# Row maxima added to the attention scores by one-hot products on TensorE instead of by a transfer into the stacked operand

## What is computed

```python
x = x + causal_self_attention(layernorm(x))            # no weights, q = k = v
x = x + cross_attention(layernorm(x), ctx, bias)       # bias is (16, 16 heads, 128, 128), added to the scores
x = x + ffn_block(layernorm(x))                        # a second attention, then a mixture of 8 experts, top 1

scores = einsum("bhtd,bhsd->bhts", q, k) + bias        # cross; the ffn block's attention has no bias
probs  = softmax(scores, axis=-1)
attn   = einsum("bhts,bhsd->bhtd", probs, v)
```

## Time and profile before

| | |
|---|---|
| median of 3 runs | 578.4 us (578.15 to 583.85) |
| profiled execution | 579.9 us, its span 578.2 us |
| PE busy | 373.3 us, 65% of the span |
| PE weight loads | 318.1 us, 55% |
| DVE busy | 291.0 us, 50% |
| ACT busy | 202.9 us, 35% |
| POOL busy | 169.9 us, 29% |
| moved by DMA | 82.35 MB, mean 142 GB/s |

### The profile page before, as it was taken

The page is one execution under the profiler, slowest core; times in us unless marked ns, Lnnn a source line. Parts: engine busy times, 40 slices in busy tenths (PEclk is TensorE's granted clock), DMA queues, the critical chain, the costliest instruction groups (busy, mean ns, idle before and its releaser), DMA issues.

```text
span 578.2 us, 11981 instructions
## 1 busy us (share of the span) xinstructions
PE 373.3 (65%) x4299; PEld 318.1 (55%) x4299; DVE 291.0 (50%) x845; ACT 202.9 (35%) x414; POOL 169.9 (29%) x244
## 2 busy tenths in 40 slices
PE   1285666625849696686958966486367395007995
PEld 0164444514638585675857856376356384007995
DVE  4124121215775575755757655545366274404773
ACT  1255444422324232332324333344245163003552
POOL 4222101210122222333334544123123123371543
PEclk9989777777787897987979977857788588557999
DMA  2777677888384856758544433945856421122331
GB/s 76 187 191 201 173 196 214 217 217 215 99 202 128 214 139 174 199 135 217 130 105 116 116 81 103 227 108 131 203 158 156 103 84 47 36 104 68 100 88 39
DMA packets 75335, 82.35 MB, mean 142 GB/s; under 512 B 6171, under 2 KB 61566, under 8 KB 71822
## 3 DMA queue, kind: packets, MB, share of 16 engines
q1 hardware_dynamic: 73774, 78.43, 52.8%
q0 software_dynamic: 1504, 3.16, 1.6%
HBM read 56.20 MB, written 25.51 MB: 141 GB/s over the span
## 4 chain that ended last, share of the span: by engine, by line
DMA 36%; PE 25%; SPq 18%; DVE 10%; issue 5%; POOL 4%; ACT 0%; POOLq 0%; DVEq 0%; ACTq 0%
DMA stack<-maxT 21%; DMA k_scratch<-parts 12%; PE out_bank L524 7%; PE score_bank L524 5%; SPq L257 5%; PE proj_bank L524 4%; PE score_bank L527 3%; PE max_bank L524 3%; SPq L287 3%; POOL routed_rows L507 3%; SPq L266 2%; DVE biased L920 2%; DVE rowmax L924 2%; SPq L253 2%; SPq L269 2%
## 5 line engine op out<-in xcount | busy, mean ns | idle before, releaser
L773 ACT ACTIVATE probs<-score_bank 128x512 f32<-128x512 f32 x192 | 112.2, 598 | 220.4 <-PE score_bank L524 218.7
L524 PE MATMUL score_bank<-stack 74*128 74x128 bf16 (+1 forms) x768 | 111.2, 247 | 49.8 <-DMA stack<-maxT 49.8
L524 PEld LDWEIGHTS score_bank<-stack 74*128 74x128 bf16 (+1 forms) x768 | 74.3, 113 | 64.9 <-issue 57.4
L527 PE MATMUL score_bank<-ident,bias_in 128*128 128x128 f32 x256 | 57.6, 309 | 35.9 <-DMA stack<-maxT 35.9
L524 PE MATMUL out_bank<-probs,vaug 128*32 128x128 f32 x1536 | 68.9, 336 | 0.0
L527 PEld LDWEIGHTS score_bank<-ident,bias_in 128*128 128x128 f32 x256 | 41.1, 161 | 42.1 <-issue 36.1
L429 POOL TENSOR_TENSOR att_sel<-att,in_block 128x1024 f32<-128x1024 f32 x16 | 34.3, 2144 | 89.7 <-DVE att L956 89.7
L524 PEld LDWEIGHTS out_bank<-probs,vaug 128*32 128x32 f32 x1536 | 50.6, 134 | 10.4 <-issue 5.0
L524 PE MATMUL score_bank<-causal,identb 128*128 128x512 bf16 x64 | 29.8, 465 | 40.9 <-DMA stack<-k_scratch 40.9
L381 POOL TENSOR_SCALAR vareps<-meanvar 128x2 f32<-128x2 f32 x32 | 7.1, 223 | 164.4 <-DVE meanvar L869 164.3
L945 DVE COPY maxT<-finish_bank 128x128 bf16<-128x128 bf16 x32 | 7.1, 222 | 93.4 <-PE finish_bank L589 93.4
(11 more groups left out here) (141 smaller groups left out, 642.5 us busy)
## 6 DMA issues: line engine op xcount, KB each, us to landing
k_scratch<-parts SPq DMA_DIRECT2D x72, 192.0 KB, 3.2
stack<-q_scratch SPq DMA_DIRECT2D x24, 576.0 KB
stack<-k_scratch SPq DMA_DIRECT2D x24, 576.0 KB
q_scratch<-parts SPq DMA_DIRECT2D x24, 192.0 KB, 2.9
bias_in<-in_w SPq DMA_DIRECT2D x16, 256.0 KB, 3.9
routed_rows<-filler SPq DMA_DIRECT2D x2, 1028.0 KB, 8.9
vaug<-routed_rows SPq DMA_DIRECT2D x23, 64.5 KB, 1.8
parts<-routed_rows SPq DMA_DIRECT2D x23, 64.0 KB, 2.1
```

Of the source, the lines that this page charges most:

```text
L524: return nc.tensor.matmul(o, lhsT, rhs, start=start, stop=stop, **kw)
L527: return nc.tensor.matmul(o, src, ident[:], start=True, stop=stop, is_transpose=True)
L773: nc.scalar.activation(probs[:, b % 2, g, :], sbk[g % 2][:], ACT.Exp, scale=1.0 if layer(b) == CROSS else SCALE).then_inc(s_p, 1)
```

## The change

The stack keeps its 72 rows; the two rows for the maxima and for ones go, with `max_rows` on SP, the three transfers of ones, and their semaphores. In place of `ones_row` there is `pick`, 128 x 16 x 128 in bf16: for head h it is one in the rows h and h + 16 and zero elsewhere. POOL makes it with a memset and two selects. In `scores`, for each head of a cross or ffn item, a second product follows that of the stack: `pick[:, head, :]` as weights and `maxT[:, b % 2, :]`, all 128 rows of it, as the moving operand, added into the same bank. PE waits for `s_maxT` in place of the transfer's semaphore, and once for `pick`. DVE, before it writes a buffer of `maxT` again, waits for the scores that read it.

```diff
-MROWS = ROWS + 2
-        stack = sb("stack", [MROWS, NSTACK, 2, NH, PAIR], bf16)
+        stack = sb("stack", [ROWS, NSTACK, 2, NH, PAIR], bf16)
-        ones_row = sb("ones_row", [128, PAIR], bf16)
+        pick = sb("pick", [128, NH, S], bf16)
...
-            def max_rows(b):
-                wait(sp, s_maxT, b - B + 1)
-                sp.dma_start(stack[ROWS:MROWS, b // 2 % NSTACK, 0, :, b % 2 * S:(b % 2 + 1) * S],
-                             maxT[0:2 * NH, b % 2, :]).then_inc(s_maxrow[b % 2], 16)
...
-                if b == 6:
-                    sp.wait_ge(s_pool_const, 1)
-                    for i in range(NSTACK):
-                        sp.dma_start(stack[ROWS:MROWS, i, 1, :, :],
-                                     ones_row[0:2, :].unsqueeze(1).to_broadcast([2, NH, PAIR])).then_inc(s_ones, 16)
...
-                if FIRST_CROSS <= b + 1 < NB:
-                    max_rows(b + 1)
...
-            nc.gpsimd.memset(ones_row[:], 1.0).then_inc(s_pool_const, 1)
+            nc.gpsimd.memset(pick[:], 0.0).then_inc(s_pool_const, 1)
...
+                nc.gpsimd.affine_select(out=pick[:], in_=pick[:], compare_op=ALU.not_equal, fill=1.0, base=0,
+                                        pattern=[[-1, NH], [0, S]], channel_multiplier=1).then_inc(s_pool_const, 1)
+                pool.wait_ge(s_pool_const, 13)
+                nc.gpsimd.affine_select(out=pick[:], in_=pick[:], compare_op=ALU.not_equal, fill=1.0, base=-NH,
+                                        pattern=[[-1, NH], [0, S]], channel_multiplier=1).then_inc(s_pool_const, 1)
...
             def scores(b, g):
                 i, s, bk, kind = b // 2 % NSTACK, b % 2, sbk[g % 2], layer(b)
-                depth = ROWS if kind == SELF else MROWS
...
                     if kind != SELF:
-                        pe.wait_ge(s_maxrow[b % 2], 16 * ((b - B) // 2 + 1))
+                        pe.wait_ge(s_maxT, b - B + 1)
                     if b == FIRST_CROSS:
-                        pe.wait_ge(s_ones, 16 * NSTACK)
+                        pe.wait_ge(s_pool_const, 14)
...
-                    last = mm(o, stack[0:depth, i, 1, head, s * S:(s + 1) * S],
-                              stack[0:depth, i, 0, head, s * S:(s + 1) * S], start=kind == FFN,
-                              stop=kind != SELF or h == G - 1)
+                    last = mm(o, stack[:, i, 1, head, s * S:(s + 1) * S], stack[:, i, 0, head, s * S:(s + 1) * S],
+                              start=kind == FFN, stop=kind == SELF and h == G - 1)
+                    if kind != SELF:
+                        last = mm(o, pick[:, head, :], maxT[:, b % 2, :], start=False)
...
             def take_maxT(b):
                 dve.wait_ge(s_mtr, b - B + 1)
-                wait(dve, s_maxrow[b % 2], 16 * ((b - B) // 2))
+                wait(dve, s_e, NG * (b - 1))
                 nc.vector.tensor_copy(maxT[:, b % 2, :], fb[:].bitcast(bf16)[:, 0:128]).then_inc(s_maxT, 1)
```

More of the change, by code:

```diff
@@ L162, in build @@
         s_stack = [sem(f"stack_loaded{i}") for i in range(NSTACK)]
-        s_ones = sem("ones_in_stack")
-        s_maxrow = [sem(f"max_rows_in_stack{i}") for i in range(2)]
         s_pool_const = sem("pool_constants")
```

## The result

| | before | after |
|---|---|---|
| median | 581.1 us (4 runs beside the new ones) | 530.1 us (528.6 to 536.2) |
| ratio | | 0.916, 95% interval 0.905 to 0.927 |
| span of the profiled execution | 578.2 us | 528.9 us |
| mean granted clock of PE | 0.81 | 0.88 |

The account below looks back on a forecast made before the run. The prediction took PE's waits for the late row-maxima transfer into the stack as the bound. Cross -25, FFN -42, rows of ones -1.3, last slots +1 made -67 to -68 from 578.2: 510 us, range 494 to 535.

Parts of the forecast that it names:

- PE is slower than priced: Rival: clock stays at 0.82 to 0.86, all sixteen products count; cross pair 21.5, FFN 15.7, 535 us; chance 0.14.
- FFN stage: Seven pairs of 20.2 us become 14.2 us, PE waiting for the stack some 2 us per pair: 42 us less.
- removed wait in the cross stage: Long slot part falls from 15.33 to 10.0 us; a pair with products takes 19.7 us; eight pairs 25 us less.
- the stack takes over the wait: Rival: earlier bias loads delay the loop's writes and reads; cross pair about 22 us, FFN 17, 550 us; chance 0.13.
- price of the products: 512 added products at 0.056 us each, 28.7 us in all; eight of a slot's sixteen count, 0.45 us per slot.
- depth costs nothing: New products 128 deep cost as much as those 72 deep, since weight loads take 109 ns against 113 ns.
- the circle: PE score maxima, DVE row maxima, PE transpose; in the FFN stage, with products, 12.4 us per pair.
- L = 18.2: FFN loop from exponential through k's write to DRAM and stack read to score maxima: 20.2 us less 2.0.
- P = 14.2: FFN pair in us: two pairs span L + 12.4 - 2.2 = 28.4; 15.2 if L stays, 12.4 if hidden.
- overlap of 2.2 us: FFN stage: PE work from `scores` to the first score maxima at full clock, taken off the loop's two-pair span.
- rows of ones: Start of the kernel: removing three issues on SP gives 1.3 us less (0 to 2).
- Slower: Rival: added products on a PE at half clock; cross pairs 35 us, FFN 26, +90 + 43, 710 us; chance 0.03.

Follow-up runs that it names:

- experiment 3: The changed kernel with a second product, weights of zeros, beside each new one (512 more): 545.6 us, ratio 0.940 to the kernel before.
- Experiment 11: The kernel before, its row-maxima transfer kept, with 512 zero-weight products and the new waits added: 586.3 us, ratio 1.016.
- experiment 12: The changed kernel with the added products cut to 32 rows deep: 691.4 us, ratio 1.174 to the kernel before.
- experiment 1: The changed kernel with its three 1 MB filler writes issued after SP's slot loop: 518.4 us, ratio 0.895 to the kernel before.
- experiment 5: The changed kernel, fillers after the loop, POOL doing `low_parts` before `inverse_deviation` from slot 16 on: 520.5 us, ratio 0.901 to the kernel before.
- experiment 7: The changed kernel, fillers after the loop, POOL doing `low_parts` before `inverse_deviation` from slot 34 on: 513.1 us, ratio 0.879 to the kernel before.
- experiment 8: The changed kernel, fillers in place, POOL doing `low_parts` before `inverse_deviation` from slot 34 on: 525.6 us, ratio 0.904 to the kernel before.
- experiment 9: The changed kernel with 24 products of 512 columns on PE before its stack wait in slots 36, 40, 44: 525.5 us, ratio 0.914 to the kernel before.

## Why the prediction was right or wrong

**The number: in the range, in part by luck.** The forecast's own bounds were 494 to 526, and 530.1 lies above them. The range reaches to 535 because the rival "PE is slower than priced" was taken in, and what made the time longer is for the most part not what that rival said. By the prediction's own sign, FFN pairs above 16 us, its FFN stage is wrong: five of the seven take 16.4 to 22.8 us.

**The bound and the removed wait in the cross stage: right.** The chain named the transfer, and without it a pair takes 19.0 to 19.5 us where the sum said 19.7. The long slot is 10.5 us (sum 10.45), the short one 9.0 (sum 9.3). The clock came back to 1.00. The first two pairs are shorter still (17.2 and 17.7); that is 4.5 us of the 6.5 that were gained beyond the sum. Why they are shorter wasn't looked into. The DMA share is 0.82 (0.84 was worked out) and the stack arrives in time, so the rival "the stack takes over the wait" is wrong for this stage.

**The price of the products: right.** 0.06 us in the trace, and a little over half of them on the path (experiment 3). Experiment 11 adds what the sum lacked: on a PE that often waits, added work is cheaper, by the waits that it fills and by the clock that it holds up. The claim that depth costs nothing was right from 72 to 128 rows, and would have been badly wrong downwards (experiment 12). It stood on one row of each depth above 64 and said nothing of smaller ones.

**The FFN stage: the mechanism right, its size wrong.** PE does wait for the stack's reads before the score maxima, as forecast (24.1 us in seven pairs, 3.4 each, for some 2), and the pairs without a stall take 12.6 to 12.8 us, where the sum had 12.4 for the circle. The step that failed is the length of the loop, L = 18.2 for every pair, and from it P = 14.2. Its parts:

- *An average over unlike pairs.* Three of seven loops have the filler in them. I took the mean, as if a pair with a short loop could give its slack to the next. It can't go under 12.6, and a long loop comes out in full: 20.5, 22.8 and 20.9 us. Moving the fillers away took 11 to 12 us (experiment 1). The filler was in SP's issues and in the prediction's own sentence.
- *What is late next.* The statistics on DVE came for free behind PE's stall. Once PE no longer waited, they became later than the middle parts, and `low_parts` on POOL, which stands behind them, started 2.7 us late. This is worth 7 us of the stage beside the moved fillers (111.8 to 104.9), 12 if it is done from slot 16 on, and 4 without that move (experiments 5, 7, 8). With the fillers moved and the order from slot 16 on, four FFN pairs in a row take 13.6 to 14.3 us (experiment 5), the 14.2 of the sum.
- *The first pairs.* Slots 32 and 33 still carry the output projection of cross items. The first pair took 16.4 us and the second 17.3 with a stall of 2.2. The sum gave them 14.2 each: 5 us.
- *The clock behind a stall.* The overlap of 2.2 us was taken at the full level throughout. The section behind a long stall ran at 0.62 and took 8.8 us. Shown in the rows, not settled in the total (experiment 9).

**The rows of ones: not settled.** 1.3 us less were forecast, and between the two profiled executions the self stage ended 0.5 us later. But it ends at 143.8 to 147.1 us in the four traces of kernels with the rows of ones and at 143.1 to 145.1 in the ten without, so a term of 1.3 us can't be read from one pair of traces; the two groups rather speak for a gain. The issue of `q_scratch` took over the place behind the full queue, as said (5.47 us at 70.20). The memset (1.8 us) and the two selects (2.0 us each) on POOL, priced at no cost, show none.

**The rivals.** "PE is slower than priced" falls for the cross stage with experiment 3 and a clock of 1.00. In the FFN stage its condition on the clock did hold: the mean there is 0.86, by the stretches at the half level behind the stalls, not by dearer products. "Slower" is wrong here. (Its sum is also wrong by some 8 us: cross pairs of 35 us are 98 us more than today's, not 90.) Experiment 12 has pairs about as long as it priced, 25 to 36 us in the cross stage for 35 and 25 to 28 in the FFN stage for 26, but only in part by its mechanism: the clock is low there, and each step is longer as well.

## What to carry to other kernels

A small transfer between two engines, on the path and in the shadow of bulk traffic, can be far dearer than its bytes: here 56 to 59 us for 32 transfers of 8 KB, against 6 to 15 us for 512 matmuls that do the same, and ACT's queue recovered only 14 to 18 us of it. When a wait is taken away, treat the slots one by one and not by their mean: look at which of them has extra traffic between a write and the read that needs it, and which in-order engine did work for free behind the wait. Then move that: here two reorderings brought 16 us more, a third of what the change itself had brought.

## What the runs showed of the hardware

- A stream that switches between products 72 and 32 rows deep loses the overlap of its weight loads: 0.15 to 0.16 us per step for 0.06 at the full clock, 150 us over the kernel, and a mean clock of 0.66 in 30 us with PE never idle in the records. Products 72 and 128 deep alternate without loss. Whether it is the depth itself or the change between the two was not tried.
- A transfer of 8 KB on a queue of its own took 6.2 to 8.7 us behind 2 MB of reads and bias issued on another, 11.2 us behind a filler and reads, and 2.6 us behind writes, at a DMA share of 1.02.
- The issue of a transfer directly behind a 1 MB bias load was held back for 5.5 us on SP.
- 512 matmuls added to a PE that often waited cost 6 to 9 us, not the 29 of their spacing; PE's idle time fell by 9 and 7 us in the two stages and the mean granted clock rose by 0.05 and 0.10. On a PE that hardly waited in the cross stage they cost 15 us.
